# Attention with a mixture of experts: the values of a key block in two parts, at two places of TensorE's queue

## What is computed

```python
Q, K, V = (heads of layernorm(x) @ W.T + b)                 # (2, 16, 2048, 16)
scores = einsum('bhqd,bhkd->bhqk', Q, K) / sqrt(16)
A = softmax(scores)
out = einsum('bhqk,bhkd->bhqd', 0.6 * A + 0.4 * L, V)        # L: a fixed band of 7 diagonals
x = x + out @ Wo.T + bo
x = x + experts(layernorm(x))                                # top 2 of 4 experts
```

## Time and profile before

| | us |
|---|---|
| median of 3 runs | 2297.64 (2287.59 to 2301.25) |
| the profiled execution | 2309.88, its span 2308.1 |
| busy in the span: TensorE matmul, VectorE, ScalarE | 2121.2 (92%), 1648.1 (71%), 1340.9 (58%) |
| first and last values matmul of `attend` | 144.8 and 1631 |

### The profile page before, as it was taken

One profiled execution on the slowest core, in us unless ns is written; L12 is line 12 of the kernel. 1 busy time (PEld: TensorE's weight loads), 2 busy tenths in 40 slices (PEclk: granted clock), 3 DMA queues, 4 the chain that ended last, 5 costly groups with the idle time before them and its releaser, 6 DMA issues. The chain is left out here.

```text
span 2308.1 us, 40692 instructions
## 1 busy us (share of the span) xinstructions
PE 2121.2 (92%) x12492; PEld 1113.0 (48%) x12492; DVE 1648.1 (71%) x2081; ACT 1340.9 (58%) x2478; POOL 384.4 (17%) x377
## 2 busy tenths in 40 slices
PE   8879999999999999999999999998898399999997
PEld 4433333333333333333333333332587289999996
DVE  6678888877888888788888787781154246565654
ACT  3237777767777777777777677777453022222221
POOL 1350000000000000000000000000045623333333
PEclk9889999989999999999999898998799599999999
DMA  7923344334522542353344233420124267676762
GB/s 252 230 51 72 65 89 104 64 64 83 109 65 64 112 81 64 71 113 73 64 95 98 64 64 78 107 52 19 41 69 159 73 243 265 240 267 247 249 244 73
DMA packets 102070, 267.61 MB, mean 116 GB/s; under 512 B 22878, under 2 KB 45920, under 8 KB 95328
## 3 DMA queue, kind: packets, MB, share of 16 engines
q1 hardware_dynamic: 91632, 241.25, 39.6%
q0 software_dynamic: 10368, 25.45, 3.1%
HBM read 212.87 MB, written 74.20 MB: 124 GB/s over the span
## 5 line engine op out<-in xcount | busy, mean ns | idle before, releaser
L543 DVE TENSOR_REDUCE part_max<-psum_attend 128x1 f32<-128x1024 f32 x1024 | 1208.3, 1220 | 232.1 <-PE psum_attend L660 231.8
L601 ACT ACTIVATE probs<-psum_attend 128x512 f32<-128x512 f32 x2048 | 1072.4, 602 | 384.0 <-PE psum_attend L672 383.7
L672 PE MATMUL psum_attend<-score_q,score_k 50*128 50x512 f32 x2048 | 770.1, 460 | 20.8 <-ACT probs L601 18.4
L672 PEld LDWEIGHTS psum_attend<-score_q,score_k 50*128 50x128 f32 x2048 | 346.4, 192 | 636.6 <-ACT probs L601 598.0
L660 PE MATMUL psum_attend<-max_k,max_q 48*128 48x512 f32 x2048 | 574.8, 473 | 51.3 <-DVE part_max L543 44.2
L681 PE MATMUL psum_attend<-probs,v_ones 128*32 128x512 f32 x4096 | 574.2, 634 | 0.7 <-ACT probs L601 0.7
L660 PEld LDWEIGHTS psum_attend<-max_k,max_q 48*128 48x128 f32 x2048 | 252.8, 191 | 181.4 <-DVE part_max L543 160.1
L1338 ACT ACTIVATE h<-psum_experts,biases 128x512 f32<-128x512 f32 x152 | 104.8, 689 | 287.2 <-PE psum_experts L1438 267.4
L492 POOL COPY v_ones<-v_sb 128x256 f32<-128x256 f32 x32 | 12.7, 398 | 1301.1 <-PE psum_attend L681 1300.9
L1454 PE MATMUL psum_experts<-w,h_hi 128*128 128x256 f32 x1216 | 219.8, 280 | 0.0
L1454 PEld LDWEIGHTS psum_experts<-w,h_hi 128*128 128x128 f32 x1216 | 195.8, 188 | 12.5
(11 more groups left out here) (146 smaller groups left out, 1261.4 us busy)
## 6 DMA issues: line engine op xcount, KB each, us to landing
w<-w_split SPq DMA_DIRECT2D x36, 2048.0 KB, 9.1
max_q<-qk_pieces SPq DMA_DIRECT2D x192, 128.0 KB, 7.4
score_k<-qk_pieces SPq DMA_DIRECT2D x192, 128.0 KB, 4.6
xs<-in_pads SPq DMA_DIRECT2D x33, 528.0 KB, 5.8
qk_pieces<-pieces SPq DMA_DIRECT2D x32, 512.0 KB, 4.7
w_split<-w_pair SPq DMA_DIRECT2D x32, 512.0 KB, 6.5
max_k<-qk_pieces SPq DMA_DIRECT2D x192, 64.0 KB, 7.5
score_q<-qk_pieces SPq DMA_DIRECT2D x192, 64.0 KB, 2.2
```

Of the source, the lines that this page charges most:

```text
L543: nc.vector.tensor_reduce(part_max[:, t, p:p + 1], ps_m[p].rearrange("q b f -> q (b f)"), axis=AXIS.X, op=ALU.max).then_inc(m_read, 1)
L601: nc.scalar.activation(probs[kb % 2][:, chunk * BLOCK:(chunk + 1) * BLOCK], ps_s[j % 3], ACT.Exp, scale=float(HD) ** -0.5).then_inc(exp_do ...
L672: nc.tensor.matmul(ps_s[j % 3], score_k[u][rows, kb * P:(kb + 1) * P], score_q[u][rows, part * BLOCK:(part + 1) * BLOCK], start=True, stop ...
```

## The change

The values of a block are done in two parts, of queries 0 to 255 and 256 to 511 of each group of 512. Each part is four matmuls of 256 columns (8 in the trace) into its half of the same bank. The first part carries the waits, and the second the signal `pv_done`. The order in a turn becomes S0 M0 S1 [transposes] V0 S2 M1 S3 V1, with the two matmuls of a maxima pair in the other order. ScalarE's and VectorE's lists stay as they are.

```diff
-            for h in range(ROW_TILES):
+            for h in (1, 0):
...
-        def values(n, kb, u):
-            pe.wait_ge(exp_done, CH * (ST * n + kb + 1))
-            if kb == 0:
-                pe.wait_ge(o_copied, n + 1)
+        def values(n, kb, u, part):
+
+            if part == 0:
+                pe.wait_ge(exp_done, CH * (ST * n + kb + 1))
+                if kb == 0:
+                    pe.wait_ge(o_copied, n + 1)
+            at = part * BLOCK // PARTS
             for j in range(BPS):
...
-            last.then_inc(pv_done, 1)
+                last = nc.tensor.matmul(ps_o[QUAD * j:QUAD * (j + 1), at:at + BLOCK // PARTS], v_ones[u][:, kb, :],
+                                        probs[kb % 2][:, j * BLOCK + at:j * BLOCK + at + BLOCK // PARTS],
+                                        start=kb == 0 and part == 0, stop=kb == ST - 1 and part == PARTS - 1)
+            if part == PARTS - 1:
+                last.then_inc(pv_done, 1)
...
                     if more_scores:
                         scores(*nxt, 1)
-                        scores(*nxt, 2)
...
-                    values(n, kb, u)
+                    values(n, kb, u, 0)
                     if more_scores:
-                        scores(*nxt, 3)
+                        scores(*nxt, 2)
                     if more_maxima:
                         if kb == 0:
                             pe.wait_ge(tok_copied, n + 1)
                         if kb == SHIFT_AT:
                             pe.wait_ge(shift_copied, n + 2)
                         maxima(g, ahead % ST, mu, 1)
+                    if more_scores:
+                        scores(*nxt, 3)
+                    values(n, kb, u, 1)
```

More of the change, by code:

```diff
@@ L380, in attend @@
     SHIFT_DMAS = PIECES * ROW_TILES
+    PARTS = 2
     ones_set = sem("ones_set")
@@ L674, in scores @@
                              ).then_inc(s_ready, 1)
-        def values(n, kb, u):
-            pe.wait_ge(exp_done, CH * (ST * n + kb + 1))
-            if kb == 0:
-                pe.wait_ge(o_copied, n + 1)
-            for j in range(BPS):
-                last = nc.tensor.matmul(ps_o[QUAD * j:QUAD * (j + 1), :], v_ones[u][:, kb, :],
-                                        probs[kb % 2][:, j * BLOCK:(j + 1) * BLOCK],
-                                        start=kb == 0, stop=kb == ST - 1)
-            last.then_inc(pv_done, 1)
+        def values(n, kb, u, part):
[4 more added lines that the diff above has]
+            at = part * BLOCK // PARTS
+            for j in range(BPS):
+                last = nc.tensor.matmul(ps_o[QUAD * j:QUAD * (j + 1), at:at + BLOCK // PARTS], v_ones[u][:, kb, :],
[3 more added lines that the diff above has]
+                last.then_inc(pv_done, 1)
         def transpose_shift(m):
```

## The result

| | before | after |
|---|---|---|
| median (lowest to highest), us, same chip | 2292.61 (2286.26 to 2301.25) | 2595.5 (2579.59 to 2647.26) |
| span of the profiled execution, us | 2308.1 | 2592.8 |
| mean granted clock of that execution | 0.944 | 0.827 |
| last values matmul of `attend`, us | 1631 | 1924 |
| time of `attend` at the lower clock, us | 146 | 790 |

The ratio is 1.130, with an interval of 1.123 to 1.137; it leaves out the execution of 2647.26, which ran over 1.5% longer than the fastest. The kernel is slower, as forecast, but by 303 us and not by 802, and nearly all of it is in `attend` (1924 - 1631 = 293). The two lowest rows come from every values matmul and from the granted clock between the first and the last of them.

What follows compares the result with a forecast made beforehand. A loop through TensorE and ScalarE was taken to bound the kernel, with no engine full. The change cuts it, but a lasting clock fall adds 879 us to 2297.6, less 80 for returns: 3100 us, range 2400 to 3210.

Steps and rivals of the forecast that it cites:

- the steady turn: In `attend`, one turn after the change: 2.48 us at full clock against 2.59, and 4.32 at 1.2 GHz.
- the part of 0.57: In the steady turn, each half of the values matmuls: 0.57 us at full clock, with bounds 0.43 and 0.99.
- The order (1, 0): In the maxima pairs: this order makes neighbouring scores and maxima run side by side, 0.67 us a stage.
- the constant 0.14 of V: In the values: time that doesn't follow the clock, taken as 0.14 of V's 0.99 us and paid by each part.
- The 4.07 "V to V" of the old turn: Steady turn before the change at 1.2 GHz: 4.07 us, read from 171.65 to 175.72.
- 10 us behind the matmuls' lengths: In the trace of head 6: the granted clock's record comes some 10 us later than the matmuls' lengths show.
- the stalls: Blocks 0 and 13: M1 waits for ScalarE's copies; extras 2.5 and 2.3 us, 5.5 a head in all, head 45.2.
- the clock falls about once in a head: At blocks 13 and 0: longer stalls let the clock fall to 1.2 GHz in nearly every head.
- rarely returning: In `attend` from head 0 on: the clock mostly stays at 1.2 GHz, 879 us for 30 heads.
- the 80 us that I took off: In the sum: 80 us subtracted from 3177 for stretches in which the clock does return, giving 3100.
- the second rival: In `attend`: the clock falls in every head and returns inside it, 2500 to 2850 us; chance 0.27.
- The third rival: In each head: waits for the copies cost no more than the extras now, gaining 2.0 us, 2232 in all; chance 0.05.

## Why the prediction was partly wrong

**Right: the steady turn.** 2.48 at full clock and 4.32 at 1.2 GHz, as summed from the earlier trace rows. V0 to V1 is 1.24, and the part of 0.57 fits: 580.63 - 580.06. Two reasons beside the sum don't hold. The order (1, 0) wasn't needed, and the constant 0.14 of V isn't paid by each matmul but once in a run of values; the sum came out since here each part is such a run. Two readings beside it were off as well, without touching the sum. The 4.07 "V to V" of the old turn was taken from S3 to S3 (171.65 to 175.72; V to V gives the same). And the granted clock doesn't come 10 us behind the matmuls' lengths. The values become longer within the row that starts at 467.28, and the clock is already below full before 468 and reads 0.50 from there:

```profile
464.00:468.00 4.00, 2.85 (x25) 0.93 (x17) 3.87 (x6) 2.77 (x6) 0.00 (x0) 0.97 0.00 0
```

That the split is what cuts the loop is shown by V whole at the first place (2.67).

**Right: the stalls.** Block 0's M1 started 1.67 behind S2 (1.7 forecast). By the medians that make up a head, block 0 cost 2.6 us more than steady turns (2.5 forecast) and block 13 2.4 (2.3 forecast), and a head took 45.31 at full clock (45.2 forecast). Early copies took this back to 42.53, so both waits are caused by the list of ScalarE that wasn't moved.

**Right: the clock falls about once in a head**, at blocks 13 and 0, and at the jump too. There are 35 falls in heads 1 to 29, where before had seven.

**Wrong: "I read it as rarely returning", with the 80 us that I took off.** The lower clock held 790 of 1780 us of `attend`, 44%, where the forecast had it nearly throughout. The term of the sum was mis-sized: of 879 us that 30 whole heads at 1.2 GHz would cost, I gave back 80, and should have given back some 650 (879 less the 232 below). The reason behind it has a true core. In the old order a fall lasts 7 us in the mean with the same waits and even with the same short matmuls (12 in before's seven falls), and in the new order 16 to 23. That its lower density is what does it is not shown, but the new order came back later, not never. I had drawn a limit between two kinds of stretches, 12 us in head 0 that returned and 50 us in the last head that didn't, and put the new turn on the wrong side of it; the last head lacks the maxima, and its TensorE really idles (41.32 busy of 50). The steady new turn at 1.2 GHz doesn't (40.00 of 40.00 above), which is what the second rival went by. Its forecast of 15 to 40 us low in each head (25 came in the mean) and 2500 to 2850 us is the case that came.

**Missing: the jump.** The text has no term for the instructions themselves. The change adds 512 of them to the loop over two heads (48884 - 40692 = 8192 in 16), and with that came 14 stalls, 45 us as they lie in after, and 8 falls, though the count alone isn't what does it (two parts at the old place). Had I read the queue of instructions on the page and asked what more instructions in the body do to it, the stall would have been a rival.

**The sum as it was.** `attend` grew by 293 us. The head at full clock gives 0.51 x 32 = 16, the 14 stalls 45, and the rest, 232, is 644 us more at the lower clock. 0.43 us for each, as in the forecast, would be 277: too much, probably since some of the 644 us are waits, which don't grow with the clock. Taken by cause instead: without the copies' waits 255 us go (2595.5 to 2340.1), and without the jump 117 (2478.6). Without both, 384 go (2211.6), which is about the sum. It is more than the 303 us that the change cost, since the new order by itself gains some 80.

**The third rival** (faster, 2232) had its condition named: all extras of a head under 5.1 us with the clock up. With early copies and no stall at the jump the extras are 42.4 - 39.7 = 2.7, and the time 2189 to 2212. It lacked only what decides whether M1 waits.

## What to carry to other kernels

When work is moved in one engine's queue, walk through the in-order lists of the engines that serve it and move their entries by as many places; two copies that were right between two exps made 255 us of difference. A stall of one us on a TensorE that is full can cost more than itself where the clock falls behind it, so price each new stall with the length of the falls that the kernel already shows, and don't take a fall for permanent while the work between the stalls is gapless. Before adding instructions to a long loop body, look at the page's instruction transfers, and again afterwards: 30 instructions out of a body took away 3.9 us at each jump.

## What the runs showed of the hardware

- A jump back in TensorE's loop stalled 2.4 to 4.4 us, in a body of 1765 instructions (before 1253). Two transfers of 16 KB came at the jump and seven more in the body. With 30 instructions fewer it didn't stall, and neither in another body of 1765. What decides between those two is open.
- The clock fell behind short idle times of TensorE in a stretch otherwise busy: before's seven falls behind two of 0.5 and 0.6 us in block 13, after's behind waits of 0.8 us (block 13) and 1.2 us (block 0), and of over 3 us at the jump. It stayed down for 3 to 61 us. With the late copies' waits and no stall at the jump, falls lasted 7 us in the mean in the old order, where a steady turn at the lower clock took 4.07, and 19 in the new one, where it took 4.32 and TensorE was busy for 40.00 of 40.00 us in the stretch shown; before's own seven had 12. What sets the moment of return in a single fall wasn't found.
- Dividing a values matmul of 512 columns into two of 256 directly behind one another costs nothing (2.61 a turn both ways). Moving them apart costs, by an estimate, 0.14 us for the further run of values: 0.57 for a part against 0.43, half of the 0.85 that follows the clock.
- Whether the upper or the lower rows of a pair come first made no difference: 2.48 a turn both ways, though with (0, 1) neighbours in the queue want the same rows.
